# Two cross-attention layers on one core: the turn of a head group's output one V block earlier on TensorE, and its copy one step earlier on ScalarE

## The chip, the cores and the metric

The kernel runs on one core of one Trainium2 chip. The metric is device time in microseconds (us), lower is better. The core's engines are TensorE (PE in the rows; its weight loads are PEld), VectorE (DVE), ScalarE (ACT), GpSimd (POOL) and SyncE (SP, which only issues DMAs here). Each engine runs its own list of instructions in order, and the lists meet only through semaphores.

## What is computed

Two attention layers, one after the other, on x of 8 batches x 100 queries x 640 channels, with a context of 8 x 722 tokens x 1024 channels. The first 77 tokens are text, the other 645 are called ip. Heads: 20 of 32 channels. Cut to what matters here:

```
# layer 0
q = x @ Wq.T;  k, v = text @ Wk.T, text @ Wv.T;  k_ip, v_ip = ip @ Wk_ip.T, ip @ Wv_ip.T
out = softmax(q k^T / sqrt(32)) v + softmax(q k_ip^T / sqrt(32)) v_ip      # per head
x = out @ Wo.T + bo + x
# layer 1: the same with its own weights, and a term added to the ip scores
text_probs = softmax(q k_text^T * scale)          # over all 640 channels at once, not per head
sem = (text_probs @ text) @ ip^T * scale          # 100 x 645 per batch
ip_probs = softmax(q_h k_ip^T * scale + 0.5 * sem) * spatial_mask
x = (text_out + ip_out) @ Wout + bout + x
```

## The kernel before, in words

Every large product is made of three fp16 products (high x high, high x low, low x high parts of both operands). Heads are taken in groups of four, so a batch has G = 5 groups, and a layer has STEPS = 40 of them. The main loop of a layer runs 40 **windows**; window u = 40 l + 5 i + g works on layer l, batch i, group g. Each engine has its own function `window(l, i, g)` in which the order of its work is written out by hand, and waits on semaphore counts in between.

In window u TensorE does the following, in this order (n = u + 1 and k = u + 2 are the groups whose V and K are being made ahead):

- V blocks: `v_tile(n, 1..5)`, 24 matmuls each (all of L586), of which 1 to 3 go to one PSUM bank and 4 and 5 to the other;
- score tiles: `score_tile(u, 0..5)`, 4 matmuls each (L719), into two PSUM banks in turn. ScalarE's `exps(u, j)` takes the exponentials of tile j twice (L1133 in fp16, L1134 in fp32). Tile j + 2 can't be computed before `exps(u, j)` has read its bank;
- the **turn** `o_turn(u - 1)`: one fp32 transpose (L750) of `osum`, the finished output of the group before, which VectorE has just normalised (`normalise`, L1812), into the PSUM tile `rows`;
- `weigh(u, 0..5)`: probabilities times V (L742, 8 matmuls each);
- parts of K for group k, and between them the four `max_scores(n, h)` (L699, L700) and `max_turn(n)` (L707), with which the maxima for the softmax of the next window are found.

ScalarE's own `o_turn` (L1140) copies the turned output out of `rows` as its fp16 high part. Then VectorE's `o_low_part` (L1600) takes the low part and frees `rows`. `v_unit(n, 0)` and `v_unit(n, 1)` (L1117 on ScalarE, L1749 on VectorE) read the first and the second V bank.

The PSUM tile **`rows`** is shared by all the small jobs: the turns, the maxima, and in layer 1 the jobs of the semantic term. They take it one after the other by the list `row_names`. A job waits until the semaphore `row_free` has counted every job ahead of it in that list (`row_ready`). In layer 1 each batch but the last makes the semantic term of the next batch in windows g = 2, 3 and 4. In g = 2 this is the job `logit`: TensorE puts the text scores into `rows` behind score tile 0 (`logits`, L760, 15 matmuls), VectorE takes their maximum (L1820, L1822), ScalarE takes their exponential behind `exps(u, 1)` (`logits`, L1156), and it is this exponential that frees `rows`. The list, for the window's middle:

```
row_names += [(("logit", "pT", "semq")[g - 2], i + 1)] if ahead and g >= 2 else []
row_names += [("oT", u - 1)] if u % STEPS else []
```

In g = 3 the job there is `pT` (freed by VectorE), in g = 4 `semq` (freed by VectorE's L1850). In layer 0, window g = 1 has a turn of the context's maxima (`ctx`) there, freed by VectorE's L1473.

Of the kernel before, what the change touches and what calls it, by code (L numbers as in the profile page):

```python
# [42 lines left out]
STEPS = B * G  # L43
# [28 lines left out]
def xattn_pair_kernel(nc, ctx_d, text_d, x_d, w_d, wq_d, wo_d, bias_d, mask_d, mask_row_d, const_d, sel_d, kd, qd, vd, cd, out_d):  # L72
    with ExitStack() as stack:
# [147 lines left out]
        def need(eng, s, n):  # L221

            if n > 0:
                eng.wait_ge(s, n)
# [63 lines left out]
        for l in range(LAYERS):  # L288
# [5 lines left out]
            for i in range(B):  # L294
                for g in range(G):
                    u = l * STEPS + i * G + g
# [20 lines left out]
        def row_done(eng, *name):  # L317

            eng.wait_ge(row_free, ROW[name] + 1)
# [210 lines left out]
        def _(pe):  # L530
# [62 lines left out]
            def ip_weights(v, a, b):  # L593
                return [lambda k, m=m: w_hl[:, m, v, k, a:b] for m in range(2)]
# [4 lines left out]
            def ips(r, a, b):  # L599
                return [lambda k, m=m: c_part(r % 2, m)[:, k, a:b] for m in range(2)]  # L600
# [76 lines left out]
            def v_tile(n, t):  # L677

                r, g, c = n // G, n % G, int(t > VA)
                if t in (1, VA + 1):  # L680
                    pe.wait_ge(k_low, 2 * n + c + 1)
                    if n % STEPS == 1:
                        pe.wait_ge(v_low, 2 * (n - 1) + c + 1)
                at = (t - 1 - c * VA) * P
                a = ODD + (t - 1) * P
                mm = pairs(banks[c][:, at:at + P], ips(r, a, a + P), ip_weights(1, g * P, (g + 1) * P))
                if t in (VA, NT - 1):
                    mm.then_inc(v_full, 1)
# [20 lines left out]
            def score_tile(u, j):  # L709

                l, r, g = u // STEPS, u // G, u % G
                if j == 0:
                    row_done(pe, "shift", u)
                    if u % STEPS == 0:
                        pe.wait_ge(sel_in, 16 * (l + 1))
                need(pe, p_high, u * NT + j - 1)
                a, b = ip_cols(j)
                for h in range(HG):
                    mm = nc.tensor.matmul(st[:, j % 2, h * S:(h + 1) * S], kp[:, u % 2, h, a:b],  # L719
                                          qp[:, r % 2, q_col(g, h):q_col(g, h) + S], start=True, stop=True)  # L720
                mm.then_inc(s_full, 1)
# [24 lines left out]
            def o_turn(u):  # L746

                pe.wait_ge(o_sum, u + 1)
                row_ready(pe, "oT", u)
                nc.tensor.transpose(rows[:, 0, 0:S], osum[:], ident[0:S, 0:S]).then_inc(row_full, 1)  # L750
# [81 lines left out]
            def window(l, i, g):  # L832

                u = l * STEPS + i * G + g
                n, k = u + 1, u + 2
                more, more2 = exists(n, l), exists(k, l)
                ahead = l and i < B - 1

                if not more:
                    last_window(l, u)  # L840
                    return
                if u % STEPS:
                    v_tile(n, 1)
                score_tile(u, 0)
                if ahead and g == 2:
                    logits(i + 1)
                if ahead and g == 3:
                    turn_probs(i + 1)
                if l == 0 and g == 1 and i < B - 1:
                    turn(cs, ctx_chain, 5 * (i + 1) + 1, "ctx", i + 1)  # L850
                if g == 1 and i == B - 1:
                    turn(os, o_chain, 5 * l + 1, "wo", l)
                v_tile(n, 2)
                score_tile(u, 1)
                if ahead and g == 4:
                    semantic(i + 1)
                v_tile(n, 3)
                score_tile(u, 2)
                v_tile(n, 4)
                score_tile(u, 3)  # L860
                if u % STEPS:
                    o_turn(u - 1)
                weigh(u, 0)
                v_tile(n, 5)
                weigh(u, 1)
                score_tile(u, 4)
                score_tile(u, 5)
                if ahead and g == 4:
                    turn_semantic(i + 1)
                weigh(u, 2)  # L870
                if ahead and g == 3:
                    text_ip(i + 1)
                late = l == 0 and g == 1 and i < B - 1
                begun, then = (3 if late or (ahead and g == 3) else 2), (5 if l else 6)
                if more2:
                    k_part(k, 0, 0, begun)
                max_scores(n, 0)
                if more2:
                    k_part(k, 0, begun, then)
                else:  # L880
                    out_tile(l, 0, 0, range(2))
                weigh(u, 3)
                max_scores(n, 1)
                if more2:
                    k_part(k, 0, then, KT), k_part(k, 1, 0, 1)
                else:
                    out_tile(l, 0, 0, range(2, 4))
                weigh(u, 4)
                max_scores(n, 2)
                last = 3 if late else 4  # L890
                if more2:
                    k_part(k, 1, 1, last)
                else:
                    out_tile(l, 0, 0, range(4, CT)), out_tile(l, 0, 1, range(2))
                weigh(u, 5)
                max_scores(n, 3)
                if more2:
                    k_part(k, 1, last, KT)
                else:
                    out_tile(l, 0, 1, range(2, CT))  # L900
                max_turn(n)
# [106 lines left out]
        def _(act):  # L1008
# [112 lines left out]
            def exps(u, j):  # L1121

                r = u // G
                if u >= STEPS:
                    act.wait_ge(s_sum, sums(u) + j + 1)
                else:
                    act.wait_ge(s_full, u * NT + (j + 1))
                low_done(act, u, j - 3)
                need(act, pv_tile, (u - 1) * NT + j + 1)
                if j == 0:  # L1130
                    scaled(act, r)
                scale = scales(r)[:, 4:5] if j == 0 else scales(r)[:, 1:2]
                nc.scalar.activation(p_hi[:, j, 0:Q4], st[:, j % 2, 0:Q4], ACT.Exp, scale=scale)  # L1133
                nc.scalar.activation(prob[:, j % 3, :], st[:, j % 2, 0:Q4], ACT.Exp, scale=scale).then_inc(p_high, 1)  # L1134

            def o_turn(u):

                row_filled(act, "oT", u)
                i, g = u // G % B, u % G
                nc.scalar.activation(o_hl[:, g, i, 0, :], rows[:, 0, 0:S], ACT.Copy).then_inc(o_hi, 1)  # L1140
# [27 lines left out]
            def window(l, i, g):  # L1168

                u, r = l * STEPS + i * G + g, l * B + i  # L1170
                n, k = u + 1, u + 2
                more, more2 = exists(n, l), exists(k, l)
                splits = iter(SLICES[4 * (g - 1):4 * g] if l == 0 and i < B - 1 and g in (1, 2) else ())
                chunks = iter(((0, 1, 2, 3), (4,))[g - 1] if i == B - 1 and g in (1, 2) else ())

                def split():
                    for k in splits:
                        split_context(r + 1, k)
                        break
                    for c in chunks:  # L1180
                        wo_high(l, c)
                        break

                if u % STEPS and more:
                    k_unit(n, 1)
                exps(u, 0)
                if l == 0 and i < B - 1 and g == 1:
                    act.wait_ge(ctx_chain, 5 * (r + 1) + 5)
                    if r >= 1:
                        act.wait_ge(c_out[(r + 1) % 2], placed(r - 1, 32))  # L1190
                    else:
                        act.wait_ge(w_low, 16)
                split()
                exps(u, 1)
                if l and i < B - 1 and g == 2:
                    logits(i + 1)
                split()
                exps(u, 2)
                if more:
                    v_unit(n, 0)  # L1200
                exps(u, 3)
                if u % STEPS:
                    o_turn(u - 1)
                split()
                if l and i < B - 1 and g == 4:
                    turn_semantic(i + 1)
                exps(u, 4)
                if more:
                    v_unit(n, 1)
                exps(u, 5)  # L1210
                split()
                if g == 1 and i < B - 1:
                    q_split(r + 1)
                if more2:
                    k_unit(k, 0)
# [980 lines left out]
```

## Time and profile before

| | |
|---|---|
| median of 3 runs | 1750.93 us (1750.36 to 1751.67) |
| the profiled execution's own time | 1750.12 us |
| its span, first to last instruction | 1748.3 us |
| TensorE busy | 1726.3 us, 99% of the span |
| VectorE, ScalarE, GpSimd busy | 1241.8, 781.7, 442.1 us |
| granted TensorE clock, mean | 1.000 |

The table is read so: the time of the profiled execution is 1.8 us above its span, and the span is where the rows of the trace lie. TensorE is the busy engine. Its instructions overlap each other, so that the distance from one start to the next says more than a busy time.

### The profile page before, as it was taken

To read this page: it belongs to the slowest core of one execution; us is meant where nothing else is said; L and a number is where in the kernel's file an instruction comes from. 1 tells how busy PE (TensorE), PEld (TensorE's weight loads), DVE (VectorE), ACT (ScalarE), POOL (GpSimd) and SP (SyncE) were. 2 spreads that over 40 slices of the span, in tenths; PEclk is the share of its full clock that TensorE was granted. 3 is DMA by queue.
4 is the path that set the end of the run, shared out by engine and by line. 5 is a ranking of instruction groups with operands and counts; after the bars stand their busy time and mean duration, and the time that the engine had idled before them with its cause. 6 is when DMAs were issued, how large, how long until landed. Compare 5 with 4: busy or idle time off the path is not lost.

```text
span 1748.3 us, 52469 instructions
## 1 busy us (share of the span) xinstructions
PE 1726.3 (99%) x22169; PEld 1405.3 (80%) x22169; DVE 1241.8 (71%) x3111; ACT 781.7 (45%) x1579; POOL 442.1 (25%) x543
## 2 busy tenths in 40 slices
PE   8999999999999999999999999999999999999998
PEld 4778888888888888887577888888888888888885
DVE  6877777777677777676845567767676767677786
ACT  3334545454545454545322344534353445345343
POOL 3034242424342424223200112212121212122121
PEclk9999999999999999999999999999999999999999
DMA  8643535343434343435146232323141323224212
GB/s 324 121 151 120 170 109 158 114 137 111 121 122 136 111 141 107 137 111 203 61 86 175 69 95 77 115 75 98 48 139 47 117 67 116 62 84 108 82 48 66
DMA packets 124161, 198.43 MB, mean 114 GB/s; under 512 B 41896, under 2 KB 110904, under 8 KB 117080
## 3 DMA queue, kind: packets, MB, share of 16 engines
q1 hardware_dynamic: 118744, 168.49, 33.3%
q10 hardware_dynamic: 5184, 26.60, 4.1%
q8 instruction: 175, 2.87, 0.7%
q14 instruction: 58, 0.48, 0.1%
HBM read 133.96 MB, written 60.88 MB: 111 GB/s over the span
## 4 chain that ended last, share of the span: by engine, by line
PE 92%; DVE 4%; DMA 2%; ACT 1%; issue 1%; POOL 1%; SPq 0%; ACTq 0%; DVEq 0%; POOLq 0%
PE proj L586 64%; PE pv L742 6%; PE st L719 5%; PE rows L699 4%; PE rows L586 3%; PE proj L538 3%; PE proj L575 2%; PE rows L700 2%; DVE wparts L1491 1%; DMA odd_both<-odd_both 1%; PE rows L787 1%; DMA k_dram<-arena 0%; DMA extra<-x_dram 0%; PE rows L750 0%; ACT arena L1134 0%
## 5 line engine op out<-in xcount | busy, mean ns | idle before, releaser
L586 PE MATMUL proj<-w_hl,cbuf 128*128 128x128 f16 x9600 | 601.0, 219 | 1.2 <-ACT odd_both L1098 1.2
L586 PE MATMUL proj<-cbuf,w_hl 128*128 128x322 f16 (+1 forms) x3840 | 591.5, 300 | 0.9 <-DVE arena L1749 0.6
L586 PEld LDWEIGHTS proj<-w_hl,cbuf 128*128 128x128 f16 x9600 | 548.5, 98 | 3.8 <-ACT odd_both L1098 1.9
L586 PEld LDWEIGHTS proj<-cbuf,w_hl 128*128 128x128 f16 x3840 | 367.6, 97 | 164.3 <-DVE arena L1749 0.7
L1394 POOL TENSOR_TENSOR arena<-arena 128x400 f16<-128x400 f32 x240 | 230.9, 962 | 855.5 <-ACT arena L1134 855.5
L1133 ACT ACTIVATE arena<-st,rs 128x400 f16<-128x400 f32 x480 | 287.1, 598 | 260.2 <-DVE st L1865 155.3
L1109 ACT ACTIVATE arena<-proj 128x323 f16<-128x323 f32 (+1 forms) x160 | 70.6, 441 | 486.2 <-PE proj L586 486.2
L1134 ACT ACTIVATE arena<-st,rs 128x400 f32<-128x400 f32 x480 | 285.9, 596 | 0.0
L1784 DVE TENSOR_TENSOR arena<-arena 128x400 f16<-128x400 f32 x240 | 147.3, 614 | 96.8 <-ACT arena L1134 93.5
L742 PEld LDWEIGHTS pv<-arena 128*128 128x128 f16 x3840 | 175.2, 97 | 22.2 <-POOL arena L1394 1.1
L742 PE MATMUL pv<-arena 128*128 128x34 f16 (+3 forms) x3840 | 192.4, 189 | 0.6 <-POOL arena L1394 0.5
L1865 DVE TENSOR_TENSOR st<-st,sem_t 128x400 f32<-128x400 f32 x240 | 134.9, 577 | 55.6 <-PE st L719 52.2
L1756 DVE TENSOR_REDUCE mx<-rows 100x1 f32<-100x77 f32 x320 | 75.3, 235 | 123.4 <-PE rows L700 123.1
L719 PE MATMUL st<-arena 128*128 128x100 f16 x1920 | 152.1, 207 | 3.9 <-ACT arena L1134 2.1
L1760 DVE CUSTOM_DVE_ANT_0 raw<-rows,raw 100x645 bf16<-100x645 f32 x160 | 131.7, 823 | 0.0
L1764 DVE TENSOR_REDUCE mx<-rows 100x1 f32<-100x645 f32 x160 | 131.0, 818 | 0.0
L699 PE MATMUL rows<-arena 96*128 96x512 f16 x320 | 121.4, 379 | 2.6 <-DVE mx L1764 1.1
L719 PEld LDWEIGHTS st<-arena 128*128 128x128 f16 x1920 | 108.7, 97 | 7.8 <-ACT arena L1134 5.0
L1739 DVE SCALAR_TENSOR_TENSOR arena<-proj,arena 128x323 f16<-128x323 f32 (+1 forms) x160 | 79.0, 494 | 48.2 <-ACT arena L1109 45.4
L700 PE MATMUL rows<-arena 96*128 96x229 f16 x320 | 84.0, 262 | 0.0
L1749 DVE SCALAR_TENSOR_TENSOR arena<-proj,arena 128x384 f16<-128x384 f32 (+1 forms) x160 | 77.2, 482 | 2.0 <-ACT arena L1117 2.0
L1117 ACT ACTIVATE arena<-proj 128x384 f16<-128x384 f32 (+1 forms) x160 | 70.9, 443 | 13.4 <-PE proj L586 13.4
(196 smaller groups left out, 1672.7 us busy)
## 6 DMA issues: line engine op xcount, KB each, us to landing
arena<-k_dram SPq DMA_DIRECT2D x240, 185.2 KB, 3.6
k_dram<-arena SPq DMA_DIRECT2D x160, 161.2 KB, 1.9
raw<-ctx_dram SPq DMA_DIRECT2D x16, 1290.0 KB, 7.7
c_dram<-cbuf SPq DMA_DIRECT2D x16, 1290.0 KB, 6.3
cbuf<-c_dram SPq DMA_DIRECT2D x14, 1290.0 KB, 7.9
cbuf<-w_dram ACTq DMA_DIRECT2D x24, 640.0 KB, 8.7
arena<-q_dram SPq DMA_DIRECT2D x48, 125.0 KB, 2.6
w_hl<-w_dram ACTq DMA_DIRECT2D x8, 640.0 KB, 12.4
```

What stands on the lines that cost most here:

```text
L586: mm = nc.tensor.matmul(out, x[a](k), w[b](k), start=(k == 0 and m == 0), stop=(k == KT - 1 and m == 2))
L699: nc.tensor.matmul(rows[:, 0, :], q, kp[0:IPO, n % 2, h, 0:512], start=True, stop=True)
L700: nc.tensor.matmul(rows[:, 1, 0:KW - 512], q, kp[0:IPO, n % 2, h, 512:KW], start=True, stop=True).then_inc(row_full, 1)
L719: mm = nc.tensor.matmul(st[:, j % 2, h * S:(h + 1) * S], kp[:, u % 2, h, a:b], qp[:, r % 2, q_col(g, h):q_col(g, h) + S], start=True, stop ...
L742: mm = nc.tensor.matmul(out, p[:, j, h * S:h * S + P], v, start=(j == 0 and h % 2 == 0 and m == 0), stop=(j == NT - 1 and h % 2 == 1 and m ...
L1133: nc.scalar.activation(p_hi[:, j, 0:Q4], st[:, j % 2, 0:Q4], ACT.Exp, scale=scale)
L1134: nc.scalar.activation(prob[:, j % 3, :], st[:, j % 2, 0:Q4], ACT.Exp, scale=scale).then_inc(p_high, 1)
L1394: nc.gpsimd.tensor_tensor(p_lo[:, j, 0:Q4], prob[:, j % 3, :], p_hi[:, j, 0:Q4], ALU.subtract).then_inc(p_low[1], 1)
L1760: last = nc.vector.tensor_tensor_reduce(out=junk, in0=rows_f[0:S, IPO:KW], in1=semq[r % 2], scale=1.0, scalar=LOWEST, op0=ALU.add, op1=ALU ...
L1764: last = nc.vector.tensor_reduce(mx[:, 1, h:h + 1], rows_f[0:S, IPO:KW], AX.X, ALU.max)
L1784: nc.vector.tensor_tensor(p_lo[:, j, 0:Q4], prob[:, j % 3, :], p_hi[:, j, 0:Q4], ALU.subtract).then_inc(p_low[0], 1)
L1865: nc.vector.tensor_tensor(tile, tile, term, ALU.add).then_inc(s_sum, 1)
```

## The change

In windows that have both a turn and a following window, TensorE's turn moves from behind score tile 3 to behind score tile 2, so that V block 4 and score tile 3 come behind it. On ScalarE the copy of the turned output moves from behind `exps(u, 3)` to behind `exps(u, 2)`, ahead of `v_unit(n, 0)`. The last window of each layer keeps both where they were. The list `row_names`, all waits and all instructions stay the same.

```
--- before.py
+++ after.py
@@ TensorE, window @@
                 v_tile(n, 3)
                 score_tile(u, 2)
+                if u % STEPS:
+                    o_turn(u - 1)
                 v_tile(n, 4)
                 score_tile(u, 3)
-                if u % STEPS:
-                    o_turn(u - 1)
                 weigh(u, 0)
@@ ScalarE, window @@
                 split()
                 exps(u, 2)
+                if more and u % STEPS:
+                    o_turn(u - 1)
                 if more:
                     v_unit(n, 0)
                 exps(u, 3)
-                if u % STEPS:
+                if not more:
                     o_turn(u - 1)
```

TensorE's list in a window g = 2 of layer 1, before, from score tile 1 to the first product with V (L742); `proj` is the V bank, `st` the score banks:

```order
L719 MATMUL st<-arena 128x100 [waits p_high]
L719 MATMUL st<-arena 128x100 x3
L586 MATMUL proj<-w_hl,cbuf 128x128 x24
L719 MATMUL st<-arena 128x100 [waits p_high]
L719 MATMUL st<-arena 128x100 x3
L586 MATMUL proj<-w_hl,cbuf 128x128 [waits k_low]
L586 MATMUL proj<-w_hl,cbuf 128x128 x23
L719 MATMUL st<-arena 128x100 [waits p_high]
L719 MATMUL st<-arena 128x100 x3
L750 MATMUL rows<-const,osum 128x100 [waits row_free,o_sum]
L742 MATMUL pv<-arena 128x132 [waits odd_placed,vt_in0,pv_read,v_low,p_low_dve]
```

and the same stretch with the change:

```order
L719 MATMUL st<-arena 128x100 [waits p_high]
L719 MATMUL st<-arena 128x100 x3
L586 MATMUL proj<-w_hl,cbuf 128x128 x24
L719 MATMUL st<-arena 128x100 [waits p_high]
L719 MATMUL st<-arena 128x100 x3
L750 MATMUL rows<-const,osum 128x100 [waits row_free,o_sum]
L586 MATMUL proj<-w_hl,cbuf 128x128 [waits k_low]
L586 MATMUL proj<-w_hl,cbuf 128x128 x23
L719 MATMUL st<-arena 128x100 [waits p_high]
L719 MATMUL st<-arena 128x100 x3
L742 MATMUL pv<-arena 128x132 [waits odd_placed,vt_in0,pv_read,v_low,p_low_dve]
```

Only L750 with its two waits has moved: V block 4 and score tile 3 (28 matmuls) now stand behind it.

ScalarE's list in such a window, before, from `exps(u, 1)` on (L1156 is the exponential of the text scores, L1140 the copy of the turned output):

```order
L1134 ACTIVATE arena<-st,rs 128x400
L1156 ACTIVATE pr<-rows,sm,rs 100x77 [waits probs,row_full]
L1133 ACTIVATE arena<-st,rs 128x400 [waits pv_tile,p_low_pool,s_sum]
L1134 ACTIVATE arena<-st,rs 128x400
L1117 ACTIVATE arena<-proj 128x12x32 [waits pv_tile,v_full]
L1133 ACTIVATE arena<-st,rs 128x400 [waits pv_tile,p_low_dve,s_sum]
L1134 ACTIVATE arena<-st,rs 128x400
L1140 ACTIVATE qo<-rows 128x100 [waits row_full]
```

and with the change:

```order
L1134 ACTIVATE arena<-st,rs 128x400
L1156 ACTIVATE pr<-rows,sm,rs 100x77 [waits probs,row_full]
L1133 ACTIVATE arena<-st,rs 128x400 [waits pv_tile,p_low_pool,s_sum]
L1134 ACTIVATE arena<-st,rs 128x400
L1140 ACTIVATE qo<-rows 128x100 [waits row_full]
L1117 ACTIVATE arena<-proj 128x12x32 [waits pv_tile,v_full]
L1133 ACTIVATE arena<-st,rs 128x400 [waits pv_tile,p_low_dve,s_sum]
L1134 ACTIVATE arena<-st,rs 128x400
```

L1140 has moved ahead of three instructions; L1156, which frees `rows` for the turn, stands where it stood.

## Rows read from the trace of the kernel before

**Rows 1.** The page, part 1: busy time and share of the span

```profile
PE 1726.3 (99%) x22169; PEld 1405.3 (80%) x22169; DVE 1241.8 (71%) x3111; ACT 781.7 (45%) x1579; POOL 442.1 (25%) x543
```

**Rows 2.** The chain that ended last, by engine

```profile
PE 92%; DVE 4%; DMA 2%; ACT 1%; issue 1%; POOL 1%; SPq 0%; ACTq 0%; DVEq 0%; POOLq 0%
```

**Rows 3.** TensorE's waits, whole span, two lines: us in total, times, longest

```profile
PE st L719 <- ACT arena L1134: 2.1, 4, 0.9
...
PE rows L699 <- DVE mx L1764: 1.1, 1, 1.1
```

**Rows 4.** Timeline, window u = 52 (layer 1, g = 2), TensorE: start us, us, instruction

```profile
1208.97 0.34 PE L719 MATMUL st<-arena 128*128 128x100 f16 x4
1209.15 1.50 PE L586 MATMUL proj<-w_hl,cbuf 128*128 128x128 f16 x24
...
1210.67 0.27 PE L750 MATMUL rows<-const,osum 100*128 100x100 f32 x1
1210.77 0.52 PE L742 MATMUL pv<-arena 128*128 128x132 f16 x8
```

**Rows 5.** Timeline, the same window, ScalarE and VectorE

```profile
1207.29 0.29 DVE L1812 TENSOR_TENSOR osum<-arena 100x128 f32<-100x128 f32 x1
...
1208.99 0.59 ACT L1134 ACTIVATE arena<-st,rs 128x400 f32<-128x400 f32 x1
1209.47 0.42 ACT L1156 ACTIVATE pr<-rows,sm,rs 100x77 f32<-100x77 f32 x1
```

**Rows 6.** All instructions of L1156: count, ns min/median/max, first and last start

```profile
L1156 ACT ACTIVATE pr<-rows,sm,rs x8: 416/418/419, 953.3 to 1592.5; 100x77 f32<-100x77 f32 x8
```

**Rows 7.** Timeline, window u = 76: ScalarE releases TensorE's score tile 5

```profile
1675.27 0.62 ACT L1134 ACTIVATE arena<-st,rs 128x400 f32<-128x400 f32 x1
1675.95 0.35 PE L719 MATMUL st<-arena 128*128 128x100 f16 x4 [0.44 <-ACT arena L1134]
```

**Rows 8.** Timeline, window u = 76, a turn and what follows it

```profile
1673.10 0.27 PE L750 MATMUL rows<-const,osum 100*128 100x100 f32 x1
1673.26 0.51 PE L742 MATMUL pv<-arena 128*128 128x132 f16 x8
```

**Rows 9.** Timeline, window u = 53 (layer 1, g = 3), all engines

```profile
1228.33 0.49 ACT L1117 ACTIVATE arena<-proj 128x384 f16<-128x384 f32 x1
1228.88 0.59 ACT L1133 ACTIVATE arena<-st,rs 128x400 f16<-128x400 f32 x1
1229.37 0.59 ACT L1134 ACTIVATE arena<-st,rs 128x400 f32<-128x400 f32 x1
...
1228.26 0.58 DVE L1865 TENSOR_TENSOR st<-st,sem_t 128x400 f32<-128x400 f32 x1 [0.94 <-PE st L719]
...
1230.09 0.51 PE L719 MATMUL st<-arena 128*128 128x100 f16 x8
```

**Rows 10.** Timeline, window u = 6 (layer 0, g = 1): ScalarE, then TensorE

```profile
250.54 0.63 ACT L1134 ACTIVATE arena<-st,rs 128x400 f32<-128x400 f32 x1
251.02 0.29 ACT L1140 ACTIVATE qo<-rows 128x100 f16<-128x100 f32 x1
251.15 0.79 ACT L1046 ACTIVATE cbuf<-raw 128x645 f16<-128x645 f32 x1
...
251.22 0.35 PE L719 MATMUL st<-arena 128*128 128x100 f16 x4
...
254.43 0.38 PE L742 MATMUL pv<-arena 128*128 128x66 f16 x8
254.79 0.39 PE L699 MATMUL rows<-arena 96*128 96x512 f16 x1
```

**Rows 11.** Timeline, window u = 54 (layer 1, g = 4), where `semq` holds `rows`

```profile
1250.51 0.89 DVE L1850 TENSOR_SCALAR raw<-rows,rs 100x645 f32<-100x645 f32 x1
...
1251.82 1.50 PE L586 MATMUL proj<-w_hl,cbuf 128*128 128x128 f16 x24
```

More of the change, by code:

```diff
@@ L858, in window @@
                 score_tile(u, 2)
+                if u % STEPS:
+                    o_turn(u - 1)
                 v_tile(n, 4)
                 score_tile(u, 3)
-                if u % STEPS:
-                    o_turn(u - 1)
                 weigh(u, 0)
@@ L1198, in window @@
                 exps(u, 2)
+                if more and u % STEPS:
+                    o_turn(u - 1)
                 if more:
@@ L1201, in window @@
                 exps(u, 3)
-                if u % STEPS:
+                if not more:
                     o_turn(u - 1)
```

## The prediction

> **What bounds the kernel now.** I read the page first. TensorE is busy for 99% of the span and the other engines for 71% at most [rows 1], and 92% of the chain that ended last lies on TensorE [rows 2]. So a change that takes no instruction away can gain only what TensorE waits, and it costs whatever new wait it gives TensorE. The view of waits came next: the two lines of it that the windows' exponentials and maxima cause are 2.1 us and 1.1 us in the whole run [rows 3]. There is nearly nothing to win. The question is then whether the moved turn finds its conditions met at its new place, and that I read from the timeline of single windows, for each kind of window (layer, and g from 0 to 4) one, since the jobs that share `rows` with the turn differ by g.
>
> **What the change removes and adds.** Nothing: the same matmuls, copies and DMAs are issued. On TensorE the turn's own slot in the stream is from its start to the next start, 1210.67 to 1210.77, 0.10 us [rows 4]. It is spent either way, behind a score tile before and after, so moving it costs 0. SyncE's and GpSimd's lists are untouched, and no DMA is issued by what moves. V block 4 and score tile 3 come 0.10 us later within the window, and from `weigh(u, 0)` on TensorE is where it was.
>
> **What the turn waits for.** It has two waits, `o_sum` and `row_free`.
>
> *`o_sum`.* VectorE has written `osum` at 1207.29 + 0.29 = 1207.58 [rows 5]. The turn's new place is where V block 4 started before, 1209.15 [rows 4]. It is 1.57 us early: cost 0.
>
> *`row_free`, windows g = 2 of layer 1.* In `row_names` the job `logit` stands ahead of the turn, and it is ScalarE's exponential L1156, behind `exps(u, 1)`, that frees `rows`. It runs from 1209.47 to 1209.89 [rows 5]. Before, the turn started at 1210.67 and was 0.78 us on the safe side. Now TensorE comes to it at 1209.15, which is 1209.89 - 1209.15 = **0.74 us too early**. Nothing ahead of L1156 is touched by the change: it stands behind `exps(u, 1)`, whose last instruction started at 1208.99, and ScalarE goes from the one to the other without a gap [rows 5]. So it can't come sooner. All of TensorE's work is queued behind the turn, V block 4 first, so that the 0.74 us are lost by the engine that bounds the kernel.
>
> From the release to TensorE's next matmul there is a lag: in window 76, `exps(u, 3)` ended at 1675.27 + 0.62 = 1675.89 and the matmul that waited for it started at 1675.95 [rows 7], 0.06 us. Then the turn itself: after an undisturbed stream its slot is 0.10 us, in window 76, where TensorE had just waited, the slot was 1673.26 - 1673.10 = 0.16 us [rows 8]. I take this 0.06 us more, since the new turn starts from a standstill. Per window: 0.74 + 0.06 + 0.06 = 0.86 us. From below it is 0.74 us (no lag, no slower start). From above, the turn's whole duration of 0.27 us [rows 4] would stand in place of its slot of 0.10, which gives 0.74 + 0.06 + 0.17 = 0.97 us.
>
> How often: L1156 runs 8 times, each within 416 to 419 ns, from 953.3 to 1592.5 [rows 6]. The first is in the preparation of layer 1, ahead of the loop, the other 7 are in the windows g = 2 of batches 0 to 6. Since TensorE streams without a wait there and the other engines follow it, all 7 are alike. Sum: 7 x 0.86 = **6.0 us**, between 7 x 0.74 = 5.2 and 7 x 0.97 = 6.8.
>
> *`row_free`, the other kinds of windows.* In g = 4 of layer 1 the job `semq` is freed by L1850, which ends at 1250.51 + 0.89 = 1251.40, and the turn's new place is 1251.82 [rows 11]: 0.42 us early, cost 0. In the others the job ahead is freed sooner still (in g = 3 by VectorE's first small copy, in layer 0 by the maxima of the context's turn, in the rest by `shift_put` at the window's start).
>
> **What ScalarE's move does.** The copy L1140 now delays `v_unit(n, 0)` and `exps(u, 3)`. Where ScalarE is busy throughout, its slot is 251.02 to 251.15, 0.13 us [rows 10]. Who waits: score tile 5 for `exps(u, 3)`.
>
> In an ordinary window of layer 1, `exps(u, 3)` ends at 1229.37 + 0.59 = 1229.96. Score tile 5 starts four matmuls behind tile 4, at 1230.09 + 0.18 (the distance of four such matmuls, [rows 4]) = 1230.27 [rows 9]. With the lag of 0.06 us the slack is 0.25 us. Now score tile 3 comes 0.10 us later. VectorE's addition for it (L1865) would end at 1228.94 instead of 1228.84. ScalarE, after copy and V bank, would be free at 1228.33 + 0.13 + 0.49 = 1228.95 [rows 9]. So `exps(u, 3)` is 0.1 us late, of 0.25: cost 0. If that cover were gone, each tenth would cost 27 windows x 0.1 = 2.7 us (34 windows 41 to 74, less the 7 of g = 2, where everything waits for the turn anyway).
>
> In windows g = 1 of layer 0 there is no cover: `exps(u, 3)` ends at 251.17 and tile 5 starts at 251.22 [rows 10]. It will be 0.13 us later. But further on TensorE waits again, for the first maximum: L742's eight matmuls start at 254.43 and take some 0.23 us, L699 starts only at 254.79 [rows 10], a wait of 0.13 us, which ends with VectorE behind ScalarE's `exps(u, 4)`. The sum of ScalarE's work ahead of `exps(u, 4)` is as before, so this wait shrinks by what the other grew: 0 in all. What is late next is nothing. In window 76 (layer 1, last batch, g = 1) tile 5 also stood waiting, for 0.44 us [rows 7], with no such second wait large enough: + 0.1 us once.
>
> VectorE's low part of the turned output gets its copy earlier, which frees `rows` and VectorE earlier in layer 1. The next users of `rows` did not wait for it, so I count 0.
>
> **The sum.** 6.0 + 0.1 = 6.1 us. On the profiled execution's own 1750.12 us that is 1756.2. The median of the three runs is 0.81 us above that execution, so I forecast 1750.93 + 6.1 = **1757.0 us**, 0.35% slower.
>
> **The rivals.**
>
> *The new wait is given back or isn't there.* For it: the list of jobs is the only thing that ties the turn to L1156, and another wait of TensorE later in the window would swallow part of it. Against it: in window 52 TensorE goes from tile to tile without a wait [rows 4], and all that it waits for L1764 in the run is 1.1 us [rows 3]. This would give 1750.9 us, or up to 1754.4 if half is swallowed. 5%.
>
> *The exponentials become late in layer 1.* If the copy cost ScalarE, ahead of `exps(u, 3)`, more than the slack, TensorE would wait before score tile 5 in 27 windows more. With the copy at the longest that stands in the rows above, 0.29 us in place of 0.13 [rows 10], `exps(u, 3)` starts at 1228.33 + 0.29 + 0.49 + 0.06 = 1229.17, 0.29 late of 0.25: 27 x 0.04 = 1.1 us, 1758.1 in all. From a slot of 0.25 us on it begins to cost. 5%, and this also holds whatever else makes ScalarE later.
> The Trainium skill, page "ScalarE: Activation LUTs", section "Rules for kernel authors", budgets about 0.3 us for each ACTIVATE and 0.83 ns per element, an estimate of 0.38 us for these 100 elements. By that rule the wait would be some 0.13 us in each of the 27 windows, 3.6 us, and the time about 1760.6 us. The row speaks against it: the copy's slot is 0.13 us.
>
> *It is no slower, or faster.* The one mechanism: the turn finds `rows` free (L1156 would have to end at 1209.1, 0.8 us sooner than it does), and the earlier copy then shortens the chains through VectorE that end TensorE's waits. All of these waits in the list are 2.1 + 1.1 = 3.2 us [rows 3], so the time would be 1747.7 at best, which is still within 0.2%. 2%, of which half for more than 0.2%.
>
> **How the numbers follow.** The forecast has 88%. Its own bounds are 5.2 + 0.1 and 6.8 + 0.1 us, 1756.2 to 1757.8. The runs shown lie within 0.8 us of their median, which goes on both sides: 1755.4 to 1758.6, and that also takes in the second rival by the rows. The bound that a measurement of this kernel can tell from no change, 0.2%, is 3.5 us. All of the forecast and of the second rival lies beyond it, 93%. Within it 6%, faster 1%.
>
> **What would show it.** In the profile after, L750 in the seven windows g = 2 of layer 1 follows the end of L1156 by 0.06 us, and TensorE's list of waits has a new line of about 7 x 0.6 to 0.8 us with L1156 as its releaser. In window 52's place V block 4 starts about 0.96 us behind score tile 2's last matmul (0.86 and the slot of 0.10). L1156 stays where it was relative to `exps(u, 1)`. The wait of VectorE's L1600 for ScalarE's L1140 gets shorter. Score tile 5 has no new waits in windows g = 0, 3, 4 of layer 1, and the granted clock stays at 1.00. The prediction is wrong if the turn in these windows starts right behind score tile 2, if L1134 shows up as a releaser some 27 times more, or if the windows of layer 0 have changed their length.

## The result, and the profile after

| | before | after |
|---|---|---|
| median of the runs timed together | 1750.93 us (7 runs, 1749.06 to 1753.39) | 1755.46 us (7 runs, 1754.36 to 1759.31) |
| ratio | | 1.0032, 95% interval 1.0021 to 1.0042 |
| span of the profiled execution | 1748.3 us | 1753.5 us |

The change makes the kernel 0.32% slower, 5.6 us by the ratio. The two medians alone differ by 4.5 us, the spans of the two profiled executions by 5.2 us. The forecast was 1757.0 us, 0.35% slower, in a range from 1755.4 to 1758.6.

TensorE's waits after (engine, what waited <- what released it: us in total, times, longest), beside [rows 3]:

```profile
PE rows L750 <- ACT pr L1156: 5.1, 7, 0.7
...
PE st L719 <- ACT arena L1134: 4.0, 11, 0.9
...
PE rows L699 <- DVE mx L1766: 0.6, 1, 0.6
```

The first line is new: the turn waits seven times for the exponential of the text scores. (In the kernel after, VectorE's lines stand two further down: L1764 is now L1766.) Window u = 52 in the timeline after, TensorE and then ScalarE, beside [rows 4, 5]:

```profile
1210.23 0.34 PE L719 MATMUL st<-arena 128*128 128x100 f16 x4
1211.30 0.28 PE L750 MATMUL rows<-const,osum 100*128 100x100 f32 x1 [0.73 <-ACT pr L1156]
1211.41 1.50 PE L586 MATMUL proj<-w_hl,cbuf 128*128 128x128 f16 x24
...
1210.26 0.58 ACT L1134 ACTIVATE arena<-st,rs 128x400 f32<-128x400 f32 x1
1210.73 0.42 ACT L1156 ACTIVATE pr<-rows,sm,rs 100x77 f32<-100x77 f32 x1
1211.22 0.59 ACT L1133 ACTIVATE arena<-st,rs 128x400 f16<-128x400 f32 x1
1211.71 0.59 ACT L1134 ACTIVATE arena<-st,rs 128x400 f32<-128x400 f32 x1
1212.19 0.25 ACT L1140 ACTIVATE qo<-rows 128x100 f16<-128x100 f32 x1
```

Score tile 2 starts at 1210.23, and 0.18 us later its four matmuls are through and the turn could start, at 1210.41. It starts at 1211.30, 0.89 us later. L1156 ends at 1210.73 + 0.42 = 1211.15. The idle time in brackets, 0.73 us, is less than the delay of the start: it counts from 1210.23 + 0.34 = 1210.57, where the row of score tile 2 ends, and that row runs on for 0.16 us after the next matmul could have started. Read the starts, not the brackets.

A second place changed, in window u = 54 (g = 4). TensorE's score tiles 4 and 5 (L719 x8) and the first transposes of the semantic term (L796), with VectorE's low part of the turned output (L1600, in the kernel after L1602), before:

```profile
1255.41 0.26 DVE L1600 TENSOR_TENSOR qo<-rows,qo 128x100 f16<-128x100 f32 x1 [0.35 <-ACT qo L1140]
...
1255.36 0.51 PE L719 MATMUL st<-arena 128*128 128x100 f16 x8
1255.82 0.62 PE L796 MATMUL rows<-const,raw 100*128 100x100 f32 x5
```

and after:

```profile
1257.24 0.25 DVE L1602 TENSOR_TENSOR qo<-rows,qo 128x100 f16<-128x100 f32 x1
...
1257.51 0.51 PE L719 MATMUL st<-arena 128*128 128x100 f16 x8
1257.86 0.61 PE L796 MATMUL rows<-const,raw 100*128 100x100 f32 x5
```

From start to start it was 0.46 us and is 0.35 us. L796 is the next user of `rows` behind the turned output. Before, VectorE freed `rows` at 1255.41 + 0.26 = 1255.67, and L796 started 0.15 us behind that; after, `rows` is free at 1257.24 + 0.25 = 1257.49, 0.37 us ahead of L796. So L796 had been waiting 0.1 us. This is a gain.

For the comparison of all kernels below I use `max_turn` (L707) as a mark of time: it is the last thing TensorE does ahead of each window, so that the distance between two of its starts is the length of a window, and from its 1st to its 40th start in layer 1 there are 39 windows of **layer 1's loop**. The rows of L707 in layer 1, of before and then of after (count, ns min/median/max, first and last start in us):

```profile
L707 PE MATMUL rows<-ident,mxh x40: 217/218/218, 978.7 to 1718.6; 100*128 100x100 f16 x40
...
L707 PE MATMUL rows<-ident,mxh x40: 217/218/218, 978.4 to 1723.8; 100*128 100x100 f16 x40
```

Layer 1's loop went from 739.9 to 745.4 us, + 5.5 us, all of the loss. A window g = 2 went from 17.83 to 18.73 us (+ 0.90), one of g = 4 from 19.09 to 18.98 us (- 0.12), and g = 0, 1 and 3 stayed within 0.01 us: 7 x 0.90 - 7 x 0.12 = 5.5. One window of the last batch, u = 76, went from 18.17 to 18.23 us. In layer 0 the seven windows g = 2 of batches 0 to 6 became shorter, six of them from 17.33 to 17.28 us, and so they are in every kernel here that has both parts of the change in layer 0.

### The profile page after: what moved, and what is told of

Read it like the earlier page. It is cut to its first block, busy times and chain, and to the rows that moved or that the text cites. A ratio compares the mean times of both kernels' runs of the same rounds, so it can differ in the third digit from the quotient of the medians.

```text
span 1753.5 us, 52469 instructions
## 1 busy us (share of the span) xinstructions
PE 1725.8 (98%) x22169; PEld 1404.4 (80%) x22169; DVE 1236.5 (71%) x3111; ACT 781.6 (45%) x1579; POOL 441.8 (25%) x543
## 4 chain that ended last, share of the span: by engine, by line
PE 87%; DVE 7%; ACT 3%; issue 2%; DMA 1%; POOL 1%; SPq 0%; ACTq 0%; DVEq 0%
PE proj L586 60%; PE pv L742 6%; PE rows L699 4%; PE st L719 4%; PE rows L586 3%; PE proj L538 3%; PE proj L575 2%; PE rows L700 2%; ACT arena L1134 1%; DVE wparts L1493 1%; ACT arena L1133 1%; DVE arena L1796 1%; PE rows L787 1%; POOL arena L1396 1%; DMA arena<-k_dram 0%
## 5 line engine op out<-in xcount | busy, mean ns | idle before, releaser
L1134 ACT ACTIVATE arena<-st,rs 128x400 f32<-128x400 f32 x480 | 286.3, 596 | 0.0
L742 PE MATMUL pv<-arena 128*128 128x34 f16 (+3 forms) x3840 | 192.1, 188 | 0.4 <-POOL arena L1396 0.4
L742 PEld LDWEIGHTS pv<-arena 128*128 128x128 f16 x3840 | 170.6, 97 | 21.8 <-POOL arena L1396 0.7
L719 PE MATMUL st<-arena 128*128 128x100 f16 x1920 | 152.1, 207 | 5.5 <-ACT arena L1134 4.0
L1766 DVE TENSOR_REDUCE mx<-rows 100x1 f32<-100x645 f32 x160 | 131.0, 819 | 0.0
L699 PE MATMUL rows<-arena 96*128 96x512 f16 x320 | 121.2, 379 | 2.1 <-DVE mx L1766 0.6
L719 PEld LDWEIGHTS st<-arena 128*128 128x128 f16 x1920 | 108.7, 97 | 9.3 <-ACT arena L1134 6.4
L1117 ACT ACTIVATE arena<-proj 128x384 f16<-128x384 f32 (+1 forms) x160 | 71.7, 448 | 13.4 <-PE proj L586 13.4
```

The source lines that it names most:

```text
L699: nc.tensor.matmul(rows[:, 0, :], q, kp[0:IPO, n % 2, h, 0:512], start=True, stop=True)
L742: mm = nc.tensor.matmul(out, p[:, j, h * S:h * S + P], v, start=(j == 0 and h % 2 == 0 and m == 0), stop=(j == NT - 1 and h % 2 == 1 and m ...
L1766: last = nc.vector.tensor_reduce(mx[:, 1, h:h + 1], rows_f[0:S, IPO:KW], AX.X, ALU.max)
```

## The experiments

The theory: the loss is the turn's wait in windows g = 2 of layer 1 for `rows`, which L1156 frees. The first rival: the loss is ScalarE's copy ahead of the first V bank, which makes the exponentials late. A second rival is a fixed price of a turn in the midst of the V blocks. Besides the time, each kernel is read by layer 1's loop, which does not share the scatter of the runs (last section). The first four experiments were timed beside 27 runs of the kernel before with a median of 1751.45 us, the others beside 15 with 1750.55 us.

| kernel | layer 1's loop, us | window g = 2 | window g = 4 | ratio to before, 95% |
|---|---|---|---|---|
| before | 739.9 | 17.83 | 19.09 | |
| after | 745.4 | 18.73 | 18.98 | 1.0032 [1.0021, 1.0042] |
| g = 2 put back | 739.1 | 17.83 | 18.98 | 0.9995 [0.9986, 1.0004] |
| only TensorE's part | 746.9 | 18.73 | 19.20 | 1.0042 [1.0029, 1.0054] |
| only ScalarE's part | 739.1 | 17.83 | 18.98 | 0.9997 [0.9988, 1.0006] |
| after, text exponential first | 739.1 | 17.83 | 18.98 | 0.9993 [0.9984, 1.0002] |
| g = 2 behind score tile 1 | 762.4 | 20.25 or 21.8 to 21.9 | 18.98 | 1.0122 [1.0106, 1.0137] |
| g = 4 put back | 746.3 | 18.73 | 19.10 | one run, no interval |
| before, text exponential first | 739.9 | 17.83 | 19.10 | one run, no interval |
| the best one | 737.8 | 17.83 | 18.98 | 0.9986 [0.9977, 0.9995] |

The windows' lengths are medians over batches 1 to 6. The loops and windows are read from one profiled execution of each kernel.

**g = 2 put back.** Both parts of the change are undone in the seven windows alone (cut, against the kernel after; the comments are added here).

```
-                if u % STEPS:
+                if u % STEPS and (not l or i == B - 1 or g != 2):
                     o_turn(u - 1)          # behind score tile 2; else behind score tile 3
...
-                if more and u % STEPS:
+                if more and u % STEPS and (not l or i == B - 1 or g != 2):
                     o_turn(u - 1)          # ScalarE, ahead of the first V bank; else behind exps(u, 3)
```

> The change, but in the seven windows g = 2 of layer 1 (batches 0 to 6) both the turn and its copy stand where they stood before. If the loss is the turn's wait for the exponential of the text scores (7 waits, 6.2 us in the trace of the changed kernel), the line of waits L750 <- L1156 is gone, the span is 1753.5 - 6.2 = 1747.3 us, and the kernel is 1.0 us faster than before, which a timing hardly tells from it. If the loss came from ScalarE's copy ahead of the first V bank in all windows, 27 of 34 windows of layer 1 still have it and the span stays above 1752 us.

Measured: 1750.64 us (11 runs) beside 1751.45 us (27 runs), the line L750 <- L1156 is gone, and layer 1's loop is 6.2 us shorter than after (745.36 to 739.14). The span was 1750.3 us and not 1747.3. The 3 us lie outside layer 1's loop: what comes ahead of layer 0's loop took 1.2 us more than in the profile after, and layer 0's loop 1.8 us more (683.9 us beside 682.1). There the waits for K were longer,

```profile
PE st L719 <- ACT arena L1136: 4.1, 11, 0.9
PE rows L699 <- DMA arena<-k_dram: 1.7, 2, 1.2
```

where before and after had 0.5 us of them. The new waits for ScalarE (4.1 us, 11 times) are there as in the changed kernel, and layer 1's loop is none the longer for them.

**Only TensorE's part.**

```
                 exps(u, 2)
-                if more and u % STEPS:
-                    o_turn(u - 1)
                 if more:
                     v_unit(n, 0)
                 exps(u, 3)
-                if not more:
+                if u % STEPS:
                     o_turn(u - 1)
```

> Only TensorE's turn is moved; ScalarE's copy stays behind the fourth pair of exponentials. By the theory of the turn's wait the whole wait of 6.2 us stands, and the 0.1 us per window g = 4 of layer 1 that the changed kernel wins (its first transpose of the semantic term no longer waits for rows) is lost, since the copy is no earlier: span 1748.3 + 6.2 = 1754.5 us, less up to 0.4 us of the first layer. By the theory of the late exponentials the loss is gone, with a span of 1748 to 1749 us.

Measured: 1758.71 us (5 runs), layer 1's loop 746.9 us, with the same seven waits:

```profile
PE rows L750 <- ACT pr L1156: 5.1, 7, 0.7
```

The first rival falls: without ScalarE's part layer 1's loop is not shorter but 1.6 us longer than with both. The expectation was 0.8 us too low there. Windows g = 4 are not just back at 19.09 us but at 19.20: score tile 3 and its exponentials come 0.10 us later behind the moved turn, the copy behind them too. In window u = 54 VectorE frees `rows` at 1263.63, L796 starts at 1263.78, again 0.15 us behind it, and it is 0.56 us from the score tiles' start to L796's (before 0.46, after 0.35). The span was 1760.3 us where 1754.5 was expected. Beside those 0.8 us, layer 0's loop was 4.3 us longer than in the profile before, 3.7 us of it in one window behind a wait of 1.9 us for K (last section), and what lies ahead of that loop was 0.7 us longer.

**Only ScalarE's part.**

```
                 v_tile(n, 4)
                 score_tile(u, 3)
+                if u % STEPS:
+                    o_turn(u - 1)
                 weigh(u, 0)
```

(and the turn behind score tile 2 taken out).

> Only ScalarE's copy is moved; TensorE's turn stays behind score tile 3, so that ScalarE has to wait for it ahead of the first V bank. By the theory of the turn's wait there is no wait of L750, and the span is that of before, 1748.3 us, within about 1 us (in layer 1 the turn ends just when ScalarE is through with the third pair, in layer 0 ScalarE stands for 0.6 us and has 0.86 us of slack, except in windows g = 1, where it is behind anyway). By the theory of the late exponentials the loss is at least that of the change, a span of 1753 us or more, with L1134 as the releaser.

Measured: 1750.79 us (11 runs), span 1748.3 us, layer 1's loop 739.1 us, 0.8 us less than before. So it is the earlier copy that wins the 0.1 us in windows g = 4, and the copy costs nothing in layer 1's loop but 0.07 us in window 76 (18.24 us). In layer 0 it does cost something by itself: the seven windows g = 2 of batches 0 to 6 are 0.07 us longer than before (17.40 us beside 17.33). For the gain in layer 1 the turn could have stayed where it was.

**After, text exponential first.**

```
+                if l and i < B - 1 and g == 2:
+                    logits(i + 1)
                 exps(u, 1)
-                if l and i < B - 1 and g == 2:
-                    logits(i + 1)
```

> The change, and in the windows g = 2 of layer 1 ScalarE takes the exponential of the text scores ahead of its second pair of exponentials, not behind it. It can start at 1207.98 in the time of the trace before, where ScalarE stands idle, and end at 1208.40, 0.75 us before the turn's new place. By the theory of the turn's wait the wait is gone with the turn still at its new place, the span is 1747.3 us or a little below. If the turn's place itself were what costs, the span would stay at 1753.5 us.

Measured: 1750.41 us (11 runs), layer 1's loop 739.1 us. The span was 1749.4 us and not 1747.3: layer 0's loop was 2.0 us longer than after, in an execution in which TensorE waited 2.1 us for K. ScalarE and then TensorE in window u = 52 of this kernel:

```profile
1209.66 0.42 ACT L1156 ACTIVATE pr<-rows,sm,rs 100x77 f32<-100x77 f32 x1 [0.23 <-DVE sm L1824]
1210.09 0.59 ACT L1133 ACTIVATE arena<-st,rs 128x400 f16<-128x400 f32 x1
...
1210.55 0.34 PE L719 MATMUL st<-arena 128*128 128x100 f16 x4
1210.73 0.27 PE L750 MATMUL rows<-const,osum 100*128 100x100 f32 x1
```

`rows` is free at 1209.66 + 0.42 = 1210.08, and the turn follows score tile 2 at once, at 1210.73. The turn stands at its new place, the wait is gone, and the loss with it. It was neither the place of the turn nor the copy, but the time at which L1156 frees `rows`. This takes the ground from the second rival too.

**Before, text exponential first**, the same edit in the kernel before, as a control.

> The kernel before, with the exponential of the text scores ahead of ScalarE's second pair of exponentials, as the only edit. It is the control for the kernel that has this and the change: nothing waits for this exponential in the kernel before, so windows g = 2 of layer 1 last 17.83 us as before, those of g = 4 19.09 us, layer 1's loop 739.9 us. If moving it won something by itself, g = 2 would be shorter.

Measured: 1750.94 us (1 run), layer 1's loop 739.9 us, windows g = 2 and g = 4 as before. The edit wins nothing by itself.

**g = 2 behind score tile 1.** A larger dose: the turn one V block earlier still, in the seven windows.

```
                 score_tile(u, 1)
                 ...
+                if ahead and g == 2:
+                    o_turn(u - 1)
                 v_tile(n, 3)
                 score_tile(u, 2)
-                if u % STEPS:
+                if u % STEPS and (not ahead or g != 2):
                     o_turn(u - 1)
```

> The change, but in the seven windows g = 2 of layer 1 TensorE's turn stands yet one V block earlier, behind score tile 1. What releases it does not move, so by the theory of the turn's wait the wait grows by V block 3 and score tile 2, 1.52 us: these windows last 18.73 + 1.52 = 20.25 us, layer 1's loop 745.4 + 7 x 1.52 = 756.0 us, the span some 1764 us. If the loss were a fixed price of a turn within the stream of V blocks, nothing would change.

Measured: 1772.56 us (4 runs), span 1772.6 us where some 1764 was expected, layer 1's loop 762.4 us, 6.4 us above the 756.0 expected. The wait grew as expected, to 2.41 us from possible to actual start, 1.52 more, and three of the seven windows last the expected 20.25 us. The other four last 21.8 to 21.9. A window of each kind, score tile 1, turn and V block 3, first one of the four and then one of the three:

```profile
1017.66 0.34 PE L719 MATMUL st<-arena 128*128 128x100 f16 x4
1020.25 0.28 PE L750 MATMUL rows<-const,osum 100*128 100x100 f32 x1 [2.25 <-ACT pr L1158]
1020.36 2.62 PE L586 MATMUL proj<-w_hl,cbuf 128*128 128x128 f16 x24
...
1117.33 0.34 PE L719 MATMUL st<-arena 128*128 128x100 f16 x4
1119.92 0.28 PE L750 MATMUL rows<-const,osum 100*128 100x100 f32 x1 [2.25 <-ACT pr L1158]
1120.03 1.50 PE L586 MATMUL proj<-w_hl,cbuf 128*128 128x128 f16 x24
```

The same 24 matmuls take 2.62 us in one and 1.50 us in the other. The stretches of this kernel with their granted clock (length, busy time and count of each engine, PEclk, DMA share, GB/s) tell why:

```profile
1015.00:1020.50 5.50, 3.25 (x65) 3.13 (x63) 4.02 (x13) 2.47 (x5) 0.63 (x1) 1.00 0.74 176
1020.60:1023.90 3.30, 3.30 (x35) 3.30 (x33) 0.54 (x1) 0.00 (x0) 0.22 (x1) 0.50 0.92 359
1024.00:1040.00 16.00, 16.00 (x229) 13.46 (x227) 12.36 (x38) 6.95 (x15) 2.60 (x4) 1.00 0.24 69
...
1117.40:1127.00 9.60, 7.35 (x130) 6.78 (x128) 5.30 (x16) 5.20 (x12) 1.90 (x2) 1.00 0.51 134
```

Behind four of the seven waits the granted clock was 0.50 (1.2 GHz) for a stretch, behind three it stayed at 1.00 (2.4 GHz). The DMA share is high in the stretch shown (0.92), but in the like stretch behind the third wait the clock is 0.50 as well at a share of 0.34. At the lower level such a window is 21.8 to 21.9 - 20.25 = 1.6 us longer, 4 x 1.6 = 6.4 us, which is the rest. The theory's part of the dose is as forecast: 7 x 1.52. The second rival falls here again, since one more V block ahead costs 1.52 us a window and not nothing.
The Trainium skill, page "TensorE: Matmul & The Clock Gate", section "HAM oscillation — how this bites in real kernels", describes this for a kernel whose waits for DMA last some 3 to 5 us: waits between groups of matmuls bring the clock down, and the matmuls behind them run at half rate. Here the trace shows the same for four of the seven waits of 2.25 us, which are shorter. After none of the waits of 0.73 us did the clock fall, 21 of them in three kernels (after, only TensorE's part, g = 4 put back).

**g = 4 put back.** The same edit as the first, with g != 4.

> The change, but in the seven windows g = 4 of layer 1 turn and copy stand where they stood before. By the theory that the earlier copy lets the first transpose of the semantic term start at once, these windows are back at 19.09 us from 18.98, those of g = 2 stay at 18.73, and layer 1's loop lasts 745.4 + 0.7 = 746.1 us. If the 0.1 us came from somewhere else, they stay at 18.98.

Measured: 1756.30 us (1 run), layer 1's loop 746.3 us, windows g = 4 at 19.10 us and g = 2 at 18.73. The gain of g = 4 comes from turn and copy in this window itself.

**The best one.** The change, the text exponential first, and in windows g = 3 of layer 1 a longer stretch of K between the first two products for the maxima:

```
-                begun, then = (3 if late or (ahead and g == 3) else 2), (5 if l else 6)
+                begun, then = (3 if late or (ahead and g == 3) else 2), (5 if l and not (ahead and g == 3) else 6)
```

> The change with the exponential of the text scores first, and in windows g = 3 of layer 1 one more step of K (3 matmuls, 0.41 us) between the first and the second product for the maxima, where TensorE waits 0.19 us for VectorE. This wait goes, the next gap is then 9 matmuls, as elsewhere: windows g = 3 last 24.25 - 0.19 = 24.06 us, layer 1's loop 739.1 - 1.3 = 737.8 us. Against before that is 2.1 us, 0.12%.

Measured: 1748.06 us (11 runs) beside 1750.55 us (15 runs), ratio 0.9986 [0.9977, 0.9995], span 1745.1 us, layer 1's loop 737.8 us, windows g = 3 at 24.06 us from 24.25. In window u = 53 TensorE goes through the place without a wait:

```profile
1237.17 1.41 PE L586 MATMUL proj<-cbuf,w_hl 128*128 128x323 f16 x9
1238.41 0.38 PE L742 MATMUL pv<-arena 128*128 128x66 f16 x8
1238.64 0.38 PE L699 MATMUL rows<-arena 96*128 96x512 f16 x1
```

From L742 to L699 it is 0.23 us, the length of its eight short matmuls; at the same place before, it was 1240.11 - 1239.70 = 0.41 us by the timeline. This version beats the kernel before by 0.14%. Against the kernel after it is 0.46% by the quotient of the two ratios; the two were not timed side by side. Of the 2.1 us, 0.8 come from the earlier copy and 1.3 from the longer stretch of K (739.1 to 737.8 us). That stretch was not tried in the kernel before alone.

## Why the prediction was right, point by point

- **Where the kernel is bound.** Right: layer 1's loop moved by what TensorE waited more and less in its windows, to 0.1 us, and nothing else moved it.
- **`row_free` in windows g = 2.** Right in place, releaser and count, shown by the two kernels that take the wait away in different ways (g = 2 put back, text exponential first) and by the larger dose. Sized at 0.86 us a window, it measured 0.90 (17.83 to 18.73): 7 x 0.90 = 6.3 us beside 6.0 forecast. In the timeline after, the turn starts 1211.30 - 1211.15 = 0.15 us behind the end of L1156, where I had put 0.06 us of lag. And V block 4 starts 0.11 us behind the turn, where I had put 0.16 us. In sum it is 0.26 us in place of 0.22. The 0.16 us were misread: in [rows 8] TensorE had not just waited. The score tile ahead of that turn is

```profile
1672.91 0.35 PE L719 MATMUL st<-arena 128*128 128x100 f16 x4
```

  and the turn follows it at 1673.10, 0.19 us later, in a full stream. Its slot of 0.16 us says nothing of a start from a standstill. That the term of 0.06 us nearly made up for the lag put too low is luck.
- **`o_sum` and the other kinds of windows.** Right: the list has no wait for L1812, and windows g = 0, 1, 3 of layer 1 kept their length. What I did not foresee is that the seven windows g = 2 of layer 0 would change: they lost 0.05 us each (one 0.09), some 0.4 us in all. In window u = 7 most of this lies between L742 and the second product for the maxima (0.26 us from start to start before, 0.23 after), once more a wait too short for the list. By my own sign ("if the windows of layer 0 have changed their length") this counts against me, though it is small.
- **TensorE's slot moves at cost 0.** Right: 1211.30 to 1211.41 behind the change, 0.11 us, beside 0.10.
- **ScalarE's copy.** Right that it costs 0 in the ordinary windows of layer 1: L1134 has 3 waits there before and after, 1.7 and 2.0 us. Window 76 became 0.06 us longer where 0.1 was forecast. In windows g = 1 of layer 0 the step went as worked out. TensorE in window u = 6 after, beside [rows 10]:

```profile
251.21 0.35 PE L719 MATMUL st<-arena 128*128 128x100 f16 x4 [0.18 <-ACT arena L1134]
...
254.42 0.38 PE L742 MATMUL pv<-arena 128*128 128x66 f16 x8
254.65 0.38 PE L699 MATMUL rows<-arena 96*128 96x512 f16 x1
```

  The wait before score tile 5 grew (it is why L1134 now has 11 waits and 4.0 us in the list), and the one before L699 is gone: from L742 to L699 it is 0.23 us and was 0.36. These windows last 18.09 us, as before (18.10).
- **The step that failed: "The next users of `rows` did not wait for it, so I count 0".** One kind of them did. In windows g = 4 of layer 1 L796 waited 0.1 us, and the earlier copy took that away: 7 x 0.12 = 0.8 us of gain, which the sum did not have. I had looked for it in the list of waits, and there it isn't: the tail of the matmul ahead covers it. Only the starts show it, 0.46 us against 0.35. The bound of 3.2 us on what a faster chain could win was read from the same list. It has the same hole, and it also leaves out 1.4 us that L719 waits for VectorE's L1779. VectorE's idle time for the copy, all but gone, was the sign of how much earlier `rows` became free. The users of L1140 that waited for it, before and after (us, times):

```profile
  DVE qo L1600: 18.6, 44
...
  DVE qo L1602: 1.9, 3
```

- **The sum.** Forecast 6.0 + 0.1; measured + 6.3 + 0.06 - 0.8, which is 5.5 us in layer 1's loop, and 5.6 us by the ratio. Two misses of opposite sign, the left-out gain the larger. The measured median, 1755.46 us, lies below the forecast's own bounds of 1756.2 to 1757.8 us. It lies in the stated range only because of the 0.8 us allowed for the scatter of the runs, 0.06 us above the lower end, and three of the seven runs are below that end. So the mechanism and the size of the wait were right, and that the range held was close to luck.
- **The rule of the Trainium skill's page "ScalarE: Activation LUTs", section "Rules for kernel authors",** would have made 27 further waits of some 0.13 us. There are none. The slot of the copy was 1212.19 to 1212.32 in window u = 52 (L1117 starts at 1212.32 in the timeline), 0.13 us as in the row, against the 0.38 us of the estimate. The copy's row lasts 0.25 us: the next instruction starts ahead of its end.

## What to carry to other kernels

Where small jobs take turns at one buffer in a fixed order, an instruction can only be moved up as far as the release of the job ahead of it, and that release may be on another engine, in one kind of window in five. Check the move against the slowest kind, and look whether the releasing instruction can go first: here one exponential moved ahead of a pair of others on ScalarE, which wins nothing alone, made the move harmless. On an engine that streams, waits of 0.1 us are found by the distance of starts and not by the list of waits.

## What the runs showed of the hardware

- The clock after a wait, as told above: 2.25 us of idle TensorE brought the granted clock from 1.00 to 0.50 in four of seven like places and left it in three, at 1.6 us each; waits of 0.73 us never did. The length of the wait alone does not tell: a wait of 1.86 us for K in the kernel with only TensorE's part was followed by the lower clock, one of 1.81 us in "after, text exponential first" was not.
- The start after a release: the fp32 transposes started 0.15 us behind the end of what released them, in three places (L750 in window 52 after, L796 in window 54 before and with only TensorE's part), the fp16 matmul of [rows 7] 0.06 us. What makes the difference was not tried.
- The scatter of this kernel's runs, 1749 to 1754 us, does not come from the loop of layer 1, which three kernels with like waits (g = 2 put back, only ScalarE's part, text exponential first) repeated within 0.1 us. In the profiles most of it lies in the first layer's loop, as TensorE's wait for K to come back through DRAM: 0.5 us in before and after, 1.7 us in the first experiment, 2.4 us in the second (longest 1.9 us), whose clock then fell as well, so that one window (u = 10) lasted 20.98 us in place of 17.28:

```profile
PE rows L699 <- DMA arena<-k_dram: 2.4, 2, 1.9
...
322.00:328.00 6.00, 4.14 (x27) 2.34 (x24) 1.88 (x4) 2.19 (x5) 0.94 (x1) 0.76 0.51 208
```

  The stretch ahead of that loop varied too, from 137.2 to 138.5 us. That the DMAs' own timing is the cause of the scatter was not tried.
